# Attention: value products in two parts, bank work at the end of a unit, and two unread products ahead of each piece

## The chip, the cores and the metric

The kernel runs on one core of one Trainium2 chip. The metric is the device time of one execution in microseconds (us), lower is better; three runs were taken of the kernel before.

## The reference, cut to what matters

The input x has 16 batches of 512 tokens with 128 features, float32. Three layers follow each other, each with a layer normalisation and a residual sum:

```python
x = x + 0.5 * ffn(layernorm(x))        # routed and shared experts
x = x + attention(layernorm(x))        # 16 heads of 8 features, 512 keys
x = x + 0.5 * ffn(layernorm(x))

def attention(x):                      # b = 16, s = 512
    q, k, v = x @ Wq.T + bq, x @ Wk.T + bk, x @ Wv.T + bv       # 16 heads of 8
    attn = softmax(einsum('bqhd,bkhd->bhqk', q, k) / sqrt(8))
    out = einsum('bhqk,bkhd->bqhd', attn * head_mask, v)
    return out @ Wo.T + bo
```

## The kernel before

The program has a setup, then `ffn`, `attention` and `ffn` one after the other; the change is in `attention` (L743) alone. It writes each engine's instructions out by hand, and semaphores hold the engines together. Nothing is planned by costs: the order is the order of the code.

**Tiling.** A batch (16 of them) is worked in 16 units `u`; a unit is a group `g = u // 4` of four heads and a block `t = u % 4` of 128 keys (or, for the maxima, of 128 queries). A unit has two halves, and a half has two heads. Scores are needed twice: once with the queries on the partitions, so that VectorE can take each row's maximum (`score_max`, L933, called M here; `take_max`, L1252), and once with the keys on the partitions, for the exponentials (`score_exp`, L919, called E here; `exponential` on ScalarE, L1093). The maxima run 8 units (`AHEAD`) before the exponentials. Each E or M of a half is two TensorE products that use 24 or 26 rows in each of two row tiles of the array; the M of a half uses the two row tiles that the E of the same half doesn't use (`HALVES`). The scores go through three PSUM buffers of two banks in turn (`score_bank`, `bank_free`, L826 to L835): the E of a half waits for the maximum of two halves ago, the M of a half for the exponential of the half before it.

**Value products.** `times_values` (L947) multiplies the four heads' exponentials of a unit with their values, each head in its own 32 columns of the array (`tile_position=(0, h * COLS)`), and sums in the PSUM bank `p_o` over the four blocks of a group. It is one unit behind E. In float32 each of the four products shows as two MATMUL records. When a group is done, ScalarE copies `p_o` out (`copy_o`, L1099), and the first value products of the next group wait for that copy (`o_copied`, L952).

**The shared bank.** All other work of TensorE goes through one PSUM bank `p_x`, in a fixed order of uses (`X_USES`): per batch three transposes of the maxima plus one for the next batch (`turn_max`, L964), four transposes of the sums `o0` to `o3` (`turn_o`, L971), `norm` (`turn_norm`, L979), `out` (`project_out`, L985), `v` (`project_v`, L912) for the next batch, and `x`, `q`, `k` (`turn_x` L897, `project_qk` L904) for the batch after that. Such a use is called a piece. Each fills the bank (`x_bank_filled`); an engine empties it (`x_bank_drained`); the next piece waits for that. `pieces` (L1012) gives each piece its unit on TensorE, `pieces` at L1114 (ScalarE) and L1296 (VectorE) the half in which it is emptied. A full batch has 14 pieces; the first has 11, the last but one 11 and the last 9 (`absent`, L802).

**TensorE's order in a unit** (`batch`, L992): E, M and the unit's piece in half 0; E, M and the value products of the unit before in half 1. From L995 on it waits, at the start of a group, for the maxima to have been packed into `q_pack` by GpSimd's DMA (`pack_max`, L1199), and at unit 8 for the packed operands of the next batch. The maxima travel `take_max`, `split_max` (GpSimd, L1188), `turn_max`, `copy_max` (ScalarE, L1087), `pack_max`. SP's queue issues loads, the packing of q and k (`pack_block`, L856) and the store.

```python
for half in range(2):
    score_exp(b, u, half)
    if there(ahead):
        score_max(ahead, v, half)
    if half == 0:
        pieces(b, u, is_first)
    elif u > 0:
        times_values(b, u - 1)
```

Of the kernel before, what the change touches and what calls it, by code (L numbers as in the profile page):

```python
# [742 lines left out]
def attention(nc, w, src, dst):  # L743
# [9 lines left out]
    with ExitStack() as ctx:  # L753
# [140 lines left out]
        def _(pe):  # L894
# [52 lines left out]
            def times_values(b, u):  # L947

                g, t = divmod(u, NT)
                pe.wait_ge(exp_ready, b.count(PAIRS, 2 * (u + 1)))  # L950
                if t == 0:
                    need(pe, o_copied, b.count(NQ, g))  # L952
                if u == 0:
# [38 lines left out]
            def batch(b, is_first, is_last):  # L992
                a, c = b.step(-1), b.step(1)
                for u in range(UNITS):
                    if u % NT == 0:  # L995
                        g = u // NT
                        pe.wait_ge(max_packed[g % 2], b.count(MAX_DMA * NQ // 2, MAX_DMA * (g // 2 + 1)))
                    ahead, v = (b, u + AHEAD) if u + AHEAD < UNITS else (c, u + AHEAD - UNITS)
                    if v == 0 and there(ahead):
                        pe.wait_ge(packed[ahead.par], ahead.half(PACK_DMA, PACK_DMA))  # L1000
                    for half in range(2):
                        score_exp(b, u, half)
                        if there(ahead):
                            score_max(ahead, v, half)
                        if half == 0:
                            pieces(b, u, is_first)
                        elif u > 0:
                            times_values(b, u - 1)
                        elif not is_first:
                            times_values(a, UNITS - 1)  # L1010

            def pieces(b, u, is_first):  # L1012
                a, c, e = b.step(-1), b.step(1), b.step(2)
                if u == 1:
                    turn_max(b, 1, uses(b, "m1"))
                if not is_first:
                    if u == 2:
                        turn_o(a, 3, uses(b, "o3"))
                    if u == 3:
                        turn_norm(uses(b, "norm"))  # L1020
                    if u == 4:
                        project_out(uses(b, "out"))
                if u == 5:
                    turn_max(b, 2, uses(b, "m2"))
                if u == 6:
                    turn_o(b, 0, uses(b, "o0"))
                if u == 7 and there(c):
                    project_v(uses(b, "v"))
                if u == 8 and there(e):
                    turn_x(e, uses(b, "x"))  # L1030
                if u == 9:
                    turn_max(b, 3, uses(b, "m3"))
                if u == 10:
                    turn_o(b, 1, uses(b, "o1"))
                if u == 11 and there(e):
                    project_qk(e, w.wq, uses(b, "q"))
                if u == 12 and there(e):
                    project_qk(e, w.wk, uses(b, "k"))
                if u == 13 and there(c):
                    turn_max(c, 0, uses(b, "m0"))  # L1040
                if u == 14:
# [17 lines left out]
            times_values(end, UNITS - 1)  # L1059
# [5 lines left out]
        def _(act):  # L1065
# [48 lines left out]
            def pieces(b, u, half, is_first):  # L1114
                a, c, e = b.step(-1), b.step(1), b.step(2)
                now = (u, half)
                if now == (1, 0) and not is_first:
                    copy_o(a, 3, uses(a, "o1") + 1)
                if now == (1, 1):
                    copy_max(b, 1, uses(b, "m1"))  # L1120
                if now == (3, 1) and not is_first:
# [3 lines left out]
                if now == (5, 1):  # L1125
                    copy_max(b, 2, uses(b, "m2"))
                if now == (8, 1) and there(e):
                    x_copy(e, uses(b, "x"))
                if now == (9, 0):
                    copy_o(b, 1, 0 if is_first else uses(b, "o3") + 1)  # L1130
                if now == (9, 1):
                    copy_max(b, 3, uses(b, "m3"))
                if now == (10, 0) and there(e):
                    x_high(e, uses(b, "x"))
                if now == (11, 1) and there(e):
                    operand(e, "q", w.bq, uses(b, "q"))
                if now == (12, 0) and there(e):
                    operand_high(e, "q", uses(b, "q"))
                if now == (12, 1) and there(e):
                    operand(e, "k", w.bk, uses(b, "k"))  # L1140
                if now == (13, 0):
                    copy_o(b, 2, uses(b, "o0") + 1)
                if now == (13, 1) and there(c):
                    copy_max(c, 0, uses(b, "m0"))
                if now == (14, 0) and there(e):
                    operand_high(e, "k", uses(b, "k"))
# [99 lines left out]
        def _(dve):  # L1246
# [49 lines left out]
            def pieces(b, now, is_first):  # L1296
                a, c, e = b.step(-1), b.step(1), b.step(2)
                if there(e):
                    if now == (2, 0):
                        norm_stats(e)  # L1300
                    if now == (3, 0):
                        norm_var(e)
                if not is_first:
                    if now == (2, 1):
                        normalise(a, NQ - 1, uses(b, "o3"))
                    if now == (4, 1):
                        residual(a, uses(b, "out"))
                if now == (6, 1):
# [3 lines left out]
                if now == (10, 1):  # L1312
                    normalise(b, 1, uses(b, "o1"))
                if now == (14, 1):
# [86 lines left out]
```

## Time and profile before

| | |
|---|---|
| median of 3 runs | 2099.72 us (2094.6 to 2109.0) |
| the profiled execution: its own time | 2100.33 us |
| its span, first to last instruction | 2098.1 us |
| TensorE busy over the span | 89% |
| VectorE, ScalarE, GpSimd busy | 71%, 59%, 42% |
| granted TensorE clock, mean of the span | 0.929 of full speed |
| attention, from about 652 to 1527 us | 875 us |

The times of single instructions come from the one profiled execution. A MATMUL record's time holds its way through the array too, so records overlap, and what a product costs the engine is read from start to start. In a timeline the bracket at the end of a line gives the engine's idle time before it and what released it; lines merged from several records say so with a count (x2). L12 is line 12 of the kernel before. The granted clock is a share of full speed: 1.00 is 2.4 GHz, 0.50 is 1.2 GHz.

### The profile page before, as it was taken

The numbers are of one execution on the slowest core, as the hardware profiler recorded it, in microseconds if no ns is written. First come the engines' busy times: TensorE is split into PE (matmuls) and PEld (weight loads), VectorE is DVE, ScalarE is ACT, GpSimd is POOL, SyncE is SP. The second block draws the span as 40 slices with busy tenths as digits, with TensorE's granted clock in tenths as the row PEclk, the third lists the DMA queues.
The fourth block names the chain that finished last, engine by engine and source line by source line (L and its number), as shares of the span: only waits on it lengthen the run. The fifth ranks groups of instructions, "written<-read, shape, count | busy, mean of one in ns | idle before, by whom it ended". The sixth has DMA issues, their size and how long they took to land. (4 is left out here: it accounts for less than half of the span.)

```text
span 2098.1 us, 30450 instructions
## 1 busy us (share of the span) xinstructions
PE 1860.1 (89%) x9600; PEld 1108.9 (53%) x9600; DVE 1496.2 (71%) x2379; ACT 1232.2 (59%) x1914; POOL 887.4 (42%) x875
## 2 busy tenths in 40 slices
PE   3999999999937898999999988888859999999999
PEld 2777777777812333333333333333247777777777
DVE  4767777687517878777787777887447768776775
ACT  3566455555513767666676667776635565556654
POOL 2566555655621222222222222221125565556655
PEclk9999999999955989888888889998879999999999
DMA  2000000000032323222223223222010000000000
GB/s 91 21 11 31 27 24 30 10 30 10 16 59 33 47 47 47 47 42 39 41 44 44 41 41 40 53 44 35 12 36 21 31 11 31 20 30 10 30 14 16
DMA packets 43167, 68.57 MB, mean 33 GB/s; under 512 B 9916, under 2 KB 11444, under 8 KB 43060
## 3 DMA queue, kind: packets, MB, share of 16 engines
q1 hardware_dynamic: 38256, 65.15, 15.7%
q0 software_dynamic: 4096, 1.08, 0.3%
q8 instruction: 58, 0.95, 0.2%
q10 hardware_dynamic: 708, 0.98, 0.1%
q14 instruction: 49, 0.40, 0.1%
HBM read 28.36 MB, written 12.58 MB: 20 GB/s over the span
## 5 line engine op out<-in xcount | busy, mean ns | idle before, releaser
L1259 DVE TENSOR_REDUCE attn_neg_max<-attn_p_score 128x2 f32<-128x1024 f32 x512 | 624.8, 1223 | 211.2 <-PE attn_p_score L941 209.1
L572 POOL TENSOR_TENSOR ffn_hid_low<-ffn_hidden,ffn_hid_high 128x512 fp32r<-128x512 f32 x448 | 580.6, 1298 | 454.9 <-ACT ffn_hid_high L512 454.2
L1096 ACT ACTIVATE attn_exps<-attn_p_score 128x1024 f32<-128x1024 f32 x512 | 519.8, 1025 | 286.6 <-PE attn_p_score L927 284.6
L512 ACT ACTIVATE ffn_hid_high<-ffn_hidden 128x512 fp32r<-128x512 f32 x448 | 281.0, 627 | 255.7 <-DVE ffn_hidden L705 254.8
L503 ACT ACTIVATE ffn_silu<-ffn_p_gate 128x512 f32<-128x512 f32 x448 | 264.0, 589 | 207.8 <-PE ffn_p_gate L375 207.5
L698 DVE TENSOR_TENSOR ffn_gated<-ffn_silu,ffn_p_up 128x512 f32<-128x512 f32 x352 | 240.6, 684 | 175.1 <-PE ffn_p_up L375 112.2
L941 PE MATMUL attn_p_score<-k_pack,q_pack 24*128 24x512 f32 x1024 | 283.2, 553 | 57.7 <-ACT attn_exps L1096 33.0
L958 PE MATMUL attn_p_o<-attn_exps,values 128*32 128x512 f32 x2048 | 312.0, 684 | 8.4 <-ACT attn_o_raw L1102 3.3
L927 PE MATMUL attn_p_score<-q_pack,k_pack 26*128 26x512 f32 x1024 | 271.2, 539 | 14.9 <-DMA q_pack<-attn_max_rows 14.6
L927 PEld LDWEIGHTS attn_p_score<-q_pack,k_pack 26*128 26x128 f32 x1024 | 101.4, 198 | 314.7 <-issue 207.5
L705 DVE TENSOR_TENSOR ffn_hidden<-ffn_gated,ffn_p_spread 128x512 f32<-128x512 f32 x352 | 241.2, 685 | 14.9 <-PE ffn_p_spread L416 4.1
L373 PE MATMUL ffn_p_y<-ffn_hid_high,down_high 128*128 128x512 f32 x448 | 186.3, 416 | 34.0 <-POOL ffn_hid_low L572 33.3
L373 PE MATMUL ffn_p_gate<-ffn_xt_high,gate_high 128*128 128x512 f32 x448 | 188.5, 421 | 0.0
L1203 POOL DMA_DIRECT2D q_pack<-attn_max_rows x128 | 74.3, 582 | 265.0 <-ACT attn_max_rows L1090 265.0
L373 PE MATMUL ffn_p_up<-ffn_xt_high,up_high 128*128 128x512 f32 x448 | 180.4, 403 | 2.9 <-DVE ffn_gated L698 2.8
L375 PE MATMUL ffn_p_up<-ffn_xt_low,up_high 128*128 128x512 f32 x448 | 177.5, 396 | 0.0
L375 PE MATMUL ffn_p_gate<-ffn_xt_low,gate_high 128*128 128x512 f32 x448 | 177.2, 396 | 0.0
L375 PE MATMUL ffn_p_y<-ffn_hid_low,down_high 128*128 128x512 f32 x448 | 177.1, 395 | 0.0
L374 PE MATMUL ffn_p_gate<-ffn_xt_high,gate_low 128*128 128x512 f32 x448 | 176.7, 394 | 0.0
L374 PE MATMUL ffn_p_up<-ffn_xt_high,up_low 128*128 128x512 f32 x448 | 176.2, 393 | 0.0
L374 PE MATMUL ffn_p_y<-ffn_hid_high,down_low 128*128 128x512 f32 x448 | 175.4, 391 | 0.0
L941 PEld LDWEIGHTS attn_p_score<-k_pack,q_pack 24*128 24x128 f32 x1024 | 103.9, 201 | 114.9 <-ACT attn_exps L1096 90.6
(146 smaller groups left out, 2220.9 us busy)
## 6 DMA issues: line engine op xcount, KB each, us to landing
q_pack<-attn_q_high SPq DMA_DIRECT2D x128, 64.0 KB
k_pack<-attn_k_high SPq DMA_DIRECT2D x128, 64.0 KB
ffn_x_in<-in_x SPq DMA_DIRECT2D x16, 256.0 KB, 2.8
ffn_x_res<-in_x SPq DMA_DIRECT2D x16, 256.0 KB, 2.8
after_ffn<-ffn_x_out SPq DMA_DIRECT2D x16, 256.0 KB, 2.0
attn_x_in<-after_ffn SPq DMA_DIRECT2D x16, 256.0 KB, 4.6
k_pack<-attn_k_low SPq DMA_DIRECT2D x64, 64.0 KB
q_pack<-attn_q_low SPq DMA_DIRECT2D x64, 64.0 KB
```

The costliest lines, as they stand in the source:

```text
L373: nc.tensor.matmul(out, weights[0], high, start=start, stop=False)
L374: nc.tensor.matmul(out, weights[1], high, start=False, stop=False)
L375: return nc.tensor.matmul(out, weights[0], low, start=False, stop=stop)
L503: nc.scalar.activation(silu[f % 2][0:n, :], p_gate[f % 2][0:n, :], ACT.Silu).then_inc(silu_ready, 1)
L512: nc.scalar.activation(hid_high[s][0:n, :], hidden[s][0:n, :], ACT.Copy).then_inc(high_ready, 1)
L572: nc.gpsimd.tensor_tensor(hid_low[s][0:n, :], hidden[s][0:n, :], hid_high[s][0:n, :].bitcast(F32), ALU.subtract).then_inc(low_ready, 1)
L705: V.tensor_tensor(hidden[slot(b, f)][:], gated[f % 2][:], p_spread[:], ALU.mult).then_inc(weighted_ready, 1)
L927: last = nc.tensor.matmul(score_bank("exp", b, n)[:, i, :], pack["k"][b.par][rows, g, t * P:(t + 1) * P], pack["q"][b.par][rows, g, :], st ...
L941: last = nc.tensor.matmul(score_bank("max", b, n)[:, j % 2, :], pack["q"][b.par][rows, g, t * P:(t + 1) * P], pack["k"][b.par][rows, g, :] ...
L958: last = nc.tensor.matmul(p_o[h * COLS:(h + 1) * COLS, :], values[b.par][:, t, g * QUAD + h, :], exps[(2 * u + h // 2) % len(exps)][:, h % ...
L1096: nc.scalar.activation(exps[n % len(exps)][:], score_bank("exp", b, n)[:], ACT.Exp, scale=inv_sqrt)\
L1259: V.tensor_reduce(neg_max[g % 2][:, j:j + 2, t], score_bank("max", b, n)[:], AX.X, ALU.max, negate=True).then_inc(max_read, 1)
```

## The change

In `attention`:

- `times_values` takes a half: the two products of heads 0 and 1 of the group come in half 0 and those of heads 2 and 3 in half 1. Each half waits for its own exponential alone; the wait for `o_copied` stands ahead of half 0.
- Every piece moves from half 0 of its unit to the end of half 1 of the unit before (L1012), behind that half's value products, and so comes half a unit earlier in the order.
- `keep_busy`, new, comes ahead of each piece of the table `at`: it waits until the bank `p_x` is empty for that piece and issues two products of 128 x 128 by 128 x 512 (fp32r) from the FFN's weights into it. Nobody reads them; the piece overwrites them.
- ScalarE, VectorE: the copies that empty the bank move half a unit or a unit forward.

Its core (of the moves on ScalarE and VectorE some are left out; the order of the rest is the same):

```diff
@@ -944,22 +944,23 @@
-            def times_values(b, u):
+            def times_values(b, u, half):
                 g, t = divmod(u, NT)
-                pe.wait_ge(exp_ready, b.count(PAIRS, 2 * (u + 1)))
-                if t == 0:
+                pe.wait_ge(exp_ready, b.count(PAIRS, 2 * u + half + 1))
+                if t == 0 and half == 0:
                     need(pe, o_copied, b.count(NQ, g))
...
-                for h in range(QUAD):
+                for h in (2 * half, 2 * half + 1):
                     last = nc.tensor.matmul(p_o[h * COLS:(h + 1) * COLS, :],
                                             values[b.par][:, t, g * QUAD + h, :],
                                             exps[(2 * u + h // 2) % len(exps)][:, h % 2, :], start=t == 0, stop=t == NT - 1,
                                             tile_position=(0, h * COLS))
-                last.then_inc(pv_done, 1)
+                if half == 1:
+                    last.then_inc(pv_done, 1)
@@ -1002,43 +1003,59 @@
                         score_exp(b, u, half)
                         if there(ahead):
                             score_max(ahead, v, half)
-                        if half == 0:
+                        if u > 0:
+                            times_values(b, u - 1, half)
+                        elif not is_first:
+                            times_values(a, UNITS - 1, half)
+                        if half == 1:
+                            keep_busy(b, u, is_first)
                             pieces(b, u, is_first)
-                        elif u > 0:
-                            times_values(b, u - 1)
-                        elif not is_first:
-                            times_values(a, UNITS - 1)
+
+            def keep_busy(b, u, is_first):
+                at = {0: "m1", 4: "m2", 5: "o0", 8: "m3", 9: "o1", 13: "o2"}
+                if not is_first:
+                    at |= {1: "o3", 2: "norm", 3: "out"}
+                if there(b, 1):
+                    at |= {6: "v", 12: "m0"}
+                if there(b, 2):
+                    at |= {7: "x", 10: "q", 11: "k"}
+                if u in at:
+                    pe.wait_ge(x_bank_drained, uses(b, at[u]))
+                    for _ in range(2):
+                        nc.tensor.matmul(p_x[:], w.up[0][:, 0:P], w.gate[0][:, 0:S], start=True, stop=True)

             def pieces(b, u, is_first):
-                if u == 1:
+                if u == 0:
                     turn_max(b, 1, uses(b, "m1"))
...
-                if u == 5:
+                if u == 4:
                     turn_max(b, 2, uses(b, "m2"))
-                if u == 6:
+                if u == 5:
                     turn_o(b, 0, uses(b, "o0"))
...
@@ -1114,36 +1132,34 @@
-                if now == (1, 0) and not is_first:
-                    copy_o(a, 3, uses(a, "o1") + 1)
-                if now == (1, 1):
+                if now == (1, 0):
+                    if not is_first:
+                        copy_o(a, 3, uses(a, "o1") + 1)
                     copy_max(b, 1, uses(b, "m1"))
-                if now == (3, 1) and not is_first:
+                if now == (3, 0) and not is_first:
                     copy_ot(uses(b, "norm"))
                 if now == (5, 0):
                     copy_o(b, 0, 0 if is_first else uses(a, "o2") + 1)
-                if now == (5, 1):
                     copy_max(b, 2, uses(b, "m2"))
-                if now == (8, 1) and there(e):
+                if now == (8, 0) and there(e):
                     x_copy(e, uses(b, "x"))
...
@@ -1296,22 +1312,22 @@
-                    if now == (2, 0):
+                    if now == (1, 0):
                         norm_stats(e)
-                    if now == (3, 0):
+                    if now == (2, 1):
                         norm_var(e)
...
-                    if now == (2, 1):
+                    if now == (2, 0):
                         normalise(a, NQ - 1, uses(b, "o3"))
-                    if now == (4, 1):
+                    if now == (4, 0):
                         residual(a, uses(b, "out"))
-                if now == (7, 1) and there(c):
+                if now == (7, 0) and there(c):
                     copy_values(c, uses(b, "v"))
...
```

## Rows read from the trace of the kernel before

**Rows 1.** The page's first line, the whole program

```profile
span 2098.1 us, 30450 instructions
```

**Rows 2.** Windows: attention, and one stretch of it (length, busy by engine, granted clock)

```profile
core 0: us, PE busy (x) PEld busy (x) DVE busy (x) ACT busy (x) POOL busy (x), PEclk, DMA share, GB/s
652.00:1527.00 875.00, 779.48 (x4822) 289.99 (x4818) 663.15 (x807) 594.13 (x736) 216.44 (x350) 0.89 0.26 40
759.00:776.10 17.10, 17.03 (x75) 5.78 (x74) 11.03 (x21) 8.45 (x11) 4.20 (x6) 0.50 0.55 69
```

**Rows 3.** Timeline, TensorE and ScalarE, a unit without a piece at full clock

```profile
1360.69 0.50 PE L927 MATMUL attn_p_score<-q_pack,k_pack 26*128 26x512 f32 x2
...
1361.23 1.94 ACT L1096 ACTIVATE attn_exps<-attn_p_score 128x1024 f32<-128x1024 f32 x2 [0.59 <-PE attn_p_score L927]
...
1362.31 0.50 PE L941 MATMUL attn_p_score<-k_pack,q_pack 24*128 24x512 f32 x2 [0.71 <-ACT attn_exps L1096]
...
1362.73 1.06 PE L958 MATMUL attn_p_o<-attn_exps,values 128*32 128x512 f32 x8
...
1363.73 0.50 PE L927 MATMUL attn_p_score<-q_pack,k_pack 26*128 26x512 f32 x2
```

**Rows 4.** Timeline, TensorE and ScalarE, around the copy of a group's sums

```profile
1342.26 1.02 ACT L1096 ACTIVATE attn_exps<-attn_p_score 128x1024 f32<-128x1024 f32 x1
...
1342.49 0.27 PE L967 MATMUL attn_p_x<-ident,attn_max_parts 128*32 128x128 f32 x1
...
1342.69 0.50 PE L927 MATMUL attn_p_score<-q_pack,k_pack 26*128 26x512 f32 x2
...
1343.18 0.59 ACT L1102 ACTIVATE attn_o_raw<-attn_p_o 128x512 f32<-128x512 f32 x1
...
1343.92 1.07 PE L958 MATMUL attn_p_o<-attn_exps,values 128*32 128x512 f32 x8
```

**Rows 5.** Timeline, TensorE, other kinds of piece at full clock

```profile
1336.15 1.16 PE L915 MATMUL attn_p_x<-wv,attn_xt 128*128 128x128 f32 x8 [0.37 <-DVE attn_o_norm L1277]
...
1337.24 0.50 PE L927 MATMUL attn_p_score<-q_pack,k_pack 26*128 26x512 f32 x2
...
1345.35 0.66 PE L975 MATMUL attn_p_x<-ident,attn_o_raw 128*128 128x128 f32 x4
...
1345.94 0.50 PE L927 MATMUL attn_p_score<-q_pack,k_pack 26*128 26x512 f32 x2
...
1348.93 0.47 PE L907 MATMUL attn_p_x<-attn_xt_high,wq_high 128*128 128x512 f32 x1 [0.47 <-DVE attn_o_norm L1277]
...
1349.24 0.40 PE L908 MATMUL attn_p_x<-attn_xt_high,wq_low 128*128 128x512 f32 x1
...
1349.47 0.40 PE L909 MATMUL attn_p_x<-attn_xt_low,wq_high 128*128 128x512 f32 x1
...
1349.80 0.50 PE L927 MATMUL attn_p_score<-q_pack,k_pack 26*128 26x512 f32 x2
```

**Rows 6.** One tile, `attn_p_o`: the value products' records

```profile
L958 PE MATMUL attn_p_o<-attn_exps,values x2048: 588/617/1063, 652.4 to 1521.4; 128*32 128x512 f32 x187
```

**Rows 7.** Timeline, TensorE, units at half clock

```profile
759.14 1.94 PE L958 MATMUL attn_p_o<-attn_exps,values 128*32 128x512 f32 x8
...
761.01 0.79 PE L927 MATMUL attn_p_score<-q_pack,k_pack 26*128 26x512 f32 x2
...
761.74 0.39 PE L967 MATMUL attn_p_x<-ident,attn_max_parts 128*32 128x128 f32 x1
...
765.51 0.79 PE L927 MATMUL attn_p_score<-q_pack,k_pack 26*128 26x512 f32 x2
```

**Rows 8.** Waits of TensorE in attention (in total, times, longest)

```profile
PE attn_p_score L927 <- DMA q_pack<-attn_max_rows: 11.2, 7, 3.2
PE attn_p_x L907 <- DVE attn_o_norm L1277: 6.6, 14, 0.5
...
PE attn_p_x L901 <- DVE values L1265: 4.8, 14, 0.4
```

**Rows 9.** Timeline, TensorE, after long idle times

```profile
1273.44 0.50 PE L927 MATMUL attn_p_score<-q_pack,k_pack 26*128 26x512 f32 x2 [2.59 <-DMA q_pack<-attn_max_rows]
...
1275.38 0.79 PE L927 MATMUL attn_p_score<-q_pack,k_pack 26*128 26x512 f32 x2
...
1513.36 1.93 PE L958 MATMUL attn_p_o<-attn_exps,values 128*32 128x512 f32 x8 [1.83 <-ACT attn_o_raw L1102]
```

More of the change, by code:

```diff
@@ L945, in score_max @@
                 last.then_inc(max_tile, 1)
-            def times_values(b, u):
+            def times_values(b, u, half):
                 g, t = divmod(u, NT)
-                pe.wait_ge(exp_ready, b.count(PAIRS, 2 * (u + 1)))
-                if t == 0:
+                pe.wait_ge(exp_ready, b.count(PAIRS, 2 * u + half + 1))
+                if t == 0 and half == 0:
                     need(pe, o_copied, b.count(NQ, g))
-                if u == 0:
+                if u == 0 and half == 0:
                     first_batch = isinstance(b.j, int) and b.k == 0
@@ L1022, in pieces @@
                         project_out(uses(b, "out"))
+                if u == 4:
+                    turn_max(b, 2, uses(b, "m2"))
                 if u == 5:
-                    turn_max(b, 2, uses(b, "m2"))
-                if u == 6:
                     turn_o(b, 0, uses(b, "o0"))
-                if u == 7 and there(c):
+                if u == 6 and there(c):
                     project_v(uses(b, "v"))
-                if u == 8 and there(e):
+                if u == 7 and there(e):
                     turn_x(e, uses(b, "x"))
+                if u == 8:
+                    turn_max(b, 3, uses(b, "m3"))
@@ L1031, in pieces @@
                 if u == 9:
-                    turn_max(b, 3, uses(b, "m3"))
-                if u == 10:
                     turn_o(b, 1, uses(b, "o1"))
+                if u == 10 and there(e):
+                    project_qk(e, w.wq, uses(b, "q"))
                 if u == 11 and there(e):
-                    project_qk(e, w.wq, uses(b, "q"))
-                if u == 12 and there(e):
                     project_qk(e, w.wk, uses(b, "k"))
-                if u == 13 and there(c):
+                if u == 12 and there(c):
@@ L1058, in _ @@
             every_batch(pe, batch)
-            times_values(end, UNITS - 1)
+            times_values(end, UNITS - 1, 0)
+            times_values(end, UNITS - 1, 1)
             turn_o(end, NQ - 1, last_uses)
@@ L1124, in pieces @@
                     copy_o(b, 0, 0 if is_first else uses(a, "o2") + 1)
-                if now == (5, 1):
                     copy_max(b, 2, uses(b, "m2"))
+                if now == (8, 0) and there(e):
+                    x_copy(e, uses(b, "x"))
                 if now == (8, 1) and there(e):
-                    x_copy(e, uses(b, "x"))
+                    x_high(e, uses(b, "x"))
                 if now == (9, 0):
                     copy_o(b, 1, 0 if is_first else uses(b, "o3") + 1)
-                if now == (9, 1):
                     copy_max(b, 3, uses(b, "m3"))
-                if now == (10, 0) and there(e):
-                    x_high(e, uses(b, "x"))
+                if now == (11, 0) and there(e):
+                    operand(e, "q", w.bq, uses(b, "q"))
                 if now == (11, 1) and there(e):
-                    operand(e, "q", w.bq, uses(b, "q"))
+                    operand_high(e, "q", uses(b, "q"))
                 if now == (12, 0) and there(e):
-                    operand_high(e, "q", uses(b, "q"))
+                    operand(e, "k", w.bk, uses(b, "k"))
                 if now == (12, 1) and there(e):
-                    operand(e, "k", w.bk, uses(b, "k"))
+                    operand_high(e, "k", uses(b, "k"))
                 if now == (13, 0):
                     copy_o(b, 2, uses(b, "o0") + 1)
[L1143 to L1146, printed above, removed]
+                    if there(c):
+                        copy_max(c, 0, uses(b, "m0"))
             begin, end = Turn(0, 0), Turn(0, NB - 1)
```

14 lines of the change are left out of this document (7 added, 7 removed).

## The prediction, made before the change was run

> **What bounds the kernel now.** The page gives a span of 2098.1 us [rows 1]; the profiled execution took 2100.33, so 2.2 us lie around the span, and its time is 0.6 above the median of 2099.72. The change touches attention alone, so I read windows next: attention takes 875 us at a mean granted clock of 0.89 [rows 2]. The clock has two levels, 1.00 and 0.50, so it stood at 0.50 for (1 - 0.89) / 0.50 = 0.22 of that time, 193 us, in stretches such as that of 17.1 us from 759.0 [rows 2].
>
> The timeline then shows what a unit waits for. In one without a piece, at full clock, E starts at 1360.69, its exponential at 1361.23 (0.54 later), M of half 1, which waits for that exponential, at 1362.31 (1.62), the value products at 1362.73 (2.04), the next unit's E at 1363.73: 3.04 us [rows 3]. So the unit is a loop through two engines: E, exponential, M, value products, E. The 1.00 us of the products is on it. In half 0 TensorE is idle for part of the 1.62 us, and most pieces lie there now. At half clock the same unit takes 765.51 - 761.01 = 4.50 us [rows 7], a loss of 0.32 of the time.
>
> Does this explain the 875 us? 256 units x 3.04 = 778; 6 us from the last value product (its record starts at 1521.4 [rows 6]); waits for the bank and for `q_pack`, 11.2 us and five of 4.8 to 6.6, some 38 together [rows 8]; and 193 x 0.32 = 62 at half clock. The sum is 884, within about 1%. I build on this loop.
>
> **Part 1, value products in two parts.** The 2048 records are 588 to 617 ns each, and eight of them (four heads, two records each) take 1.06 us from first start to last end [rows 3, 6]. One head alone, two records in a row, would take about as long, so the four heads run side by side. Two heads then take as long as four: I price a half at the 1.00 us from its start to the next E. From below, a price per head would give 0.50. I take 1.00, since the records' lengths speak for it. The half in half 0 starts when M does and is over 1.43 after E, ahead of the 1.62 at which M of half 1 can start: hidden there, as long as nothing else lies in that place. The half in half 1 costs its 1.00, as the whole did. A unit without a piece stays at 3.04.
>
> The Trainium skill weighs in here (TensorE: Matmul & The Clock Gate, Part 3: Packing small matmuls): it has packed tiles gain less than their number, 2.38 times for three column tiles. By that a group of two would be a little cheaper than one of four, and some 20 us would go from the sum (an estimate); no run here shows two alone.
>
> **Part 2, pieces at the end of half 1.** They leave the place that half 0 gave them and follow the value products, right ahead of the next E: in the loop, uncovered. Their prices, first record to next E: transposes 0.59 (1345.35 to 1345.94), `v` and `out` 1.09 (1336.15 to 1337.24), `q` and `k` 0.87 (1348.93 to 1349.80) [rows 5], maxima 0.20 (1342.49 to 1342.69) [rows 4]. Counts over 16 batches: 92 of four transposes (`o0` to `o2` 48, `o3` and `norm` 30, `x` 14), 30 of `v` and `out`, 28 of `q` and `k`, 63 of maxima. 92 x 0.59 + 30 x 1.09 + 28 x 0.87 + 63 x 0.20 = 124 us. From below 0, if the loop had slack behind the value products; rows 3 show none, so I take all of it. What goes: the 38 us of waits [rows 8], since each bank is emptied in the following half 0, on VectorE or ScalarE about 2.4 after E, and wanted at 3.04. (They are left out of the loop already, so nothing is subtracted twice.) The maxima's way through GpSimd and its two DMAs starts half a unit earlier and the four units that it has are longer, so I expect no `q_pack` wait; if that cover fails it costs the old 11 us. ScalarE's and VectorE's moved copies queue behind one exponential or one maximum, with half a unit to spare. SP's store and loads wait for events that come earlier in the order; nobody is late for them.
>
> **Part 3, two unread products ahead of each piece.** 92 + 30 + 28 + 63 = 213 pairs. A product of this kind costs 0.23 from start to start (1349.24 to 1349.47) [rows 5], 0.46 a pair: 98 us, in the loop as well. From above a pair with its own entry costs 0.31 + 0.23 = 0.54 [rows 5], 17 us more. From below 0, if it filled a wait for the bank; but those are gone, so 98.
>
> The Trainium skill (TensorEngine Tiling (Array Packing), Tiling Modes) says that changing the tiling mode drains the engine. The unread products follow column-tiled ones, an order that the trace of before lacks. By the rule some 0.2 us for each pair, about 40 us, could come on top (an estimate); by the row, whose 1.00 ends in such a change already, nothing.
>
> **Part 4, a new wait.** `copy_o` stays behind the exponential of half 0, at units 1, 5, 9 and 13, but the value products that wait for it now stand in half 0 of the same unit, ahead of E and M of half 1. The copy starts at 0.54 + 1.02 (the exponential), takes 0.59, and products follow its end by 0.15 (1343.18 + 0.59 to 1343.92) [rows 3, 4]: they start 2.30 after E instead of 0.43. Queued behind them are half 1's E and M, and with these ScalarE and VectorE. The unit becomes 2.30 + 1.00 + 0.42 + 1.00 = 4.72, 1.68 more. It happens 4 x 16 - 1 = 63 times: 106 us. Below: 0, if the copy came in time. Above: the 1.83 that such a wait took at 1513.36 [rows 9]. I take 1.68.
>
> **Part 5, the clock.** At full clock attention would take 778 + 124 + 98 + 106 + 6 = 1112 us, 237 more than 875. At half clock a unit is bound by TensorE: scores 0.73 and products 1.87 [rows 7], twice: 5.20 against 3.04, a loss of 0.42 of the time spent so. The unread products fill TensorE, but the copy waits leave it idle for 1.8 us four times a batch, and the clock fell after a wait of 2.59 (scores at 0.50 at 1273.44, 0.79 at 1275.38) and at one of 1.83 (value products 1.93 at 1513.36) [rows 9]. Also no pair stands in units 14, 15 and most of 0. So I expect half clock in some 0.12 of attention, between 0 and the 0.22 of before: 1112 / (1 - 0.12 x 0.42) = 1171 us, 296 more. 2098.1 + 296 + 2.2 = 2396; less the 0.6 to the median: **2395 us**.
>
> **Rivals.**
> - The clock is held throughout: 2100 + 237 = 2337. For it: the change adds 98 us of products over the whole array. Against: rows 9. The Trainium skill (TensorE: Matmul & The Clock Gate, HAM oscillation — how this bites in real kernels) says that sustained work keeps the clock up; by that this case would win. Chance 0.18.
> - The unread products don't do what they are for, and half clock takes 0.22 to 0.35 of attention: 1225 to 1304 us, so 2450 to 2529. Chance 0.15.
> - A half is priced by the head, 0.50. With price p attention takes 256 x (2.04 + p) + 63 x (0.68 + p) + 228 = 793 + 319 p: 952 us at 0.50, 1002 with half clock as in the forecast, so 2227. Against it are the overlapping records [rows 6]. Chance 0.14.
> - Not slower: scores of the next half start under the value products, whose halves leave half of the columns free, so that only p = 0.2 stays on the loop: 793 + 64 = 857, 18 less, 2082. It decides from p = 0.26, where 793 + 319 p is 875. For it: E and M share the array by row tiles. Against: no score starts inside a group of value products in rows 3, and pieces, pairs and copy waits still have to be won back. Chance 0.06.
>
> **How the numbers follow.** The forecast has 0.47, with a range of its own from 2340 to 2450. To hold 8 in 10 the range reaches down to the case of the price by head and up past 0.22 of half clock: 2215 to 2480. About 1% is what a measurement of this kernel tells from no change. Faster by over 1% and within 1% come from the fourth rival alone with some doubt around it: 0.04 and 0.03; slower 0.93.
>
> **What would show it.** Right: the unread products in the list of lines as 426 matmuls near 0.4 us each; value products still near 0.6 a record, in groups of four records that take 1.0; the next E some 0.5 + the piece's price after them; among TensorE's waits, value products on the copy of `p_o`, 63 times about 1.8; bank waits gone; VectorE and ScalarE with longer waits for scores; the batch near 70 us at full clock. Wrong: groups of two heads in half the time (part 1), the copy wait short or absent (part 4), units with a piece near 3 us (part 2 and the loop), granted clock in attention at 1.00 or below 0.85 (part 5), or any change in the two FFNs.

## The result, and the profile after

The change makes the kernel slower: median 2376.36 us of 4 runs (2372.57 to 2384.22) against 2101.63 of 4 runs of the kernel before, a ratio of 1.131 (95% interval 1.126 to 1.136). The forecast was 2395, with a range of 2215 to 2480. The profiled execution took 2372.57 us, its span is 2370.4. The ratios and intervals in this document leave out runs over 1.5% above the fastest of the same kernel, so they can differ a little from the quotient of two medians.

The windows of after that answer to [rows 2]: attention, and what lies on both sides of it.

```profile
core 0: us, PE busy (x) PEld busy (x) DVE busy (x) ACT busy (x) POOL busy (x), PEclk, DMA share, GB/s
652.00:1799.00 1147.00, 1038.41 (x5250) 377.67 (x5246) 665.41 (x807) 608.94 (x737) 216.68 (x350) 0.96 0.19 31
...
0.00:652.00 652.00, 552.43 (x2413) 415.37 (x2428) 432.10 (x812) 327.53 (x600) 347.23 (x276) 0.95 0.12 31
1799.00:2370.40 571.40, 527.71 (x2336) 403.48 (x2352) 400.37 (x761) 309.69 (x577) 323.81 (x249) 0.97 0.07 23
```

Attention takes 1147 us instead of 875, 272 more, and that is the whole difference: the parts beside it are 652 and 571 us long. TensorE is busy for 1038 us of it, VectorE for 665 against 663 and ScalarE for 609 against 594 [rows 2]: these two do nearly the same work and wait longer for it. The granted clock rose from 0.89 to 0.96.

The timeline of after shows one unit with all that is new. TensorE's and ScalarE's lines of unit 9, from its E (1119.56) to that of unit 10 (1125.25):

```profile
1119.56 0.49 PE L927 MATMUL attn_p_score<-q_pack,k_pack 26*128 26x512 f32 x2
...
1120.09 1.02 ACT L1114 ACTIVATE attn_exps<-attn_p_score 128x1024 f32<-128x1024 f32 x1 [0.83 <-PE attn_p_score L927]
1121.01 0.59 ACT L1120 ACTIVATE attn_o_raw<-attn_p_o 128x512 f32<-128x512 f32 x1
...
1121.75 1.05 PE L958 MATMUL attn_p_o<-attn_exps,values 128*32 128x512 f32 x4 [1.69 <-ACT attn_o_raw L1120]
...
1122.73 0.50 PE L927 MATMUL attn_p_score<-q_pack,k_pack 26*128 26x512 f32 x2
...
1123.17 1.05 PE L958 MATMUL attn_p_o<-attn_exps,values 128*32 128x512 f32 x4
...
1124.15 0.73 PE L1027 MATMUL attn_p_x<-gate_high,up_high 128*128 128x512 f32 x2
1124.72 0.60 PE L976 MATMUL attn_p_x<-ident,attn_o_raw 128*128 128x128 f32 x4
1125.25 0.50 PE L927 MATMUL attn_p_score<-q_pack,k_pack 26*128 26x512 f32 x2
```

Read it from start to start. Four records of two heads take 0.98 (1121.75 to 1122.73 and 1123.17 to 1124.15), where eight records of four heads took 1.00 [rows 3]. The first half waits 1.69 for the copy of the sums, which ScalarE starts behind its exponential. The two unread products take 0.57 and the transposes behind them 0.53, right ahead of the next E. The unit is 5.69 us long.

TensorE's waits inside attention, answering to [rows 8]:

```profile
PE attn_p_o L958 <- ACT attn_o_raw L1120: 81.2, 48, 1.7
PE attn_p_o L958 <- ACT attn_exps L1114: 24.7, 15, 1.7
PE attn_p_x L976 <- ACT attn_o_raw L1120: 0.7, 1, 0.7
```

The 48 and the 15 are the 63 waits that part 4 counted: the 15 of some 1.65 stand in unit 1, where ScalarE runs exponential and copy in the same order. The products follow the end of the copy there too (copy to 723.52, products from 723.62), though the profile names the exponential. Together they are 106 us. The waits for the bank and for `q_pack` of [rows 8] are gone.

### The profile page after: what moved, and what is told of

Same layout as the page of the kernel before. It is cut to its first block and busy times, and to the rows that moved or that the text cites. A ratio compares the mean times of both kernels' runs of the same rounds, so it can differ in the third digit from the quotient of the medians.

```text
span 2370.4 us, 31271 instructions
## 1 busy us (share of the span) xinstructions
PE 2118.6 (89%) x9995; PEld 1196.5 (50%) x10026; DVE 1497.9 (63%) x2379; ACT 1246.2 (53%) x1914; POOL 887.7 (37%) x875
## 5 line engine op out<-in xcount | busy, mean ns | idle before, releaser
L958 PE MATMUL attn_p_o<-attn_exps,values 128*32 128x512 f32 x2048 | 563.2, 629 | 106.0 <-ACT attn_o_raw L1120 81.2
L941 PE MATMUL attn_p_score<-k_pack,q_pack 24*128 24x512 f32 x1024 | 264.4, 516 | 17.4 <-DMA k_pack<-attn_k_high 12.2
L927 PE MATMUL attn_p_score<-q_pack,k_pack 26*128 26x512 f32 x1024 | 261.5, 507 | 3.3 <-DMA q_pack<-attn_max_rows 3.3
L927 PEld LDWEIGHTS attn_p_score<-q_pack,k_pack 26*128 26x128 f32 x1024 | 96.4, 185 | 309.2 <-issue 293.1
L958 PEld LDWEIGHTS attn_p_o<-attn_exps,values 128*32 128x32 f32 x2048 | 76.5, 109 | 238.6 <-ACT attn_exps L1114 127.1
L1210 POOL TENSOR_TENSOR attn_max_parts<-attn_neg_max,zeros 128x16 fp32r<-128x16 f32 x64 | 13.9, 218 | 466.8 <-DVE attn_neg_max L1275 466.8
```

What stands on the lines that cost most here:

```text
L927: last = nc.tensor.matmul(score_bank("exp", b, n)[:, i, :], pack["k"][b.par][rows, g, t * P:(t + 1) * P], pack["q"][b.par][rows, g, :], st ...
L941: last = nc.tensor.matmul(score_bank("max", b, n)[:, j % 2, :], pack["q"][b.par][rows, g, t * P:(t + 1) * P], pack["k"][b.par][rows, g, :] ...
L958: last = nc.tensor.matmul(p_o[h * COLS:(h + 1) * COLS, :], values[b.par][:, t, g * QUAD + h, :], exps[(2 * u + h // 2) % len(exps)][:, h % ...
```

## The experiments

A median is given beside its ratio to the kernel before, run on the same chip. Each window, wait and timeline comes from the one profiled execution of its kernel. In the expectations, the loop theory is the sum of parts 1 to 4 of the prediction, at a given clock; the clock theory adds what a change of the granted clock would give or take. The window of attention goes from 652 us to the end of its last residual sum on VectorE, and its columns are those of the windows of after.

### e1: without the unread products

```diff
                         if half == 1:
-                            keep_busy(b, u, is_first)
                             pieces(b, u, is_first)
```

> The change without the unread products (426 matmuls left out), all else as in the change. Loop theory: each pair stands uncovered ahead of the next scores; a pair and its piece took 1124.15 to 1125.25 in the trace of after, the pair 0.57 of it, so 213 x 0.57 = 121 us go: 2376 - 121 = 2255 us if the clock stays at its mean of 0.96 in attention. Clock theory on top: the pairs are what holds the clock; without them half clock takes about the 0.22 of attention that it had before, attention is 993 / (1 - 0.22 x 0.42) = 1094 us instead of 1147, and the time is about 2323 with a mean clock near 0.89. Rival (the pairs fill idle time): within 15 us of 2376.

Measured: 2301.58 us (2291.93 to 2307.74), ratio 1.098 (1.090 to 1.105). The 75 us that go are less than the 102 that the same products cost where the clock stays at 1.00 (e12 to e2, below): here the clock of attention falls from 0.96 to 0.93. Attention, and a stretch of it about a batch long with many falls:

```profile
652.00:1718.70 1066.70, 957.93 (x4822) 305.49 (x4818) 665.13 (x807) 608.81 (x737) 216.54 (x350) 0.93 0.21 33
...
927.00:998.00 71.00, 64.28 (x312) 20.61 (x310) 43.63 (x55) 38.71 (x48) 14.51 (x23) 0.88 0.22 35
```

The clock of 0.93 lies between the two forms of the loop theory, and so does the time. The unread products cost time and, in a kernel with the copy waits, give part of it back.

### e2: the copy of the sums ahead of the exponential

```diff
                     for half in range(2):
+                        if half == 0:
+                            group_copy(b, u, is_first)      # copy_o of units 1, 5, 9, 13
                         exponential(b, 2 * u + half)
                         pieces(b, u, half, is_first)
...
```

with the four copies taken out of `pieces`.

> The change with ScalarE's copy of a group's sums (copy_o) ahead of the exponential of half 0 instead of behind it, at units 1, 5, 9, 13. Loop theory: the sums are ready at the end of the unit before, so the copy runs beside the pair and the piece, and the 63 waits of 1.7 us go; a unit with a copy (5.69 us) becomes like one without (4.13): 63 x 1.56 = 98 us less, 2278, and some 15 less again if the half-clock stretches of 3.4 us, which come just after a copy wait, go too: 2263. Rival (the wait only takes the place of another, for the exponential or a score bank): 2360 to 2376 and the same total of TensorE waits under another name.

Measured: 2238.82 us (2237.68 to 2239.10), ratio 1.067 (1.060 to 1.074): 138 less than the change, and more than the 113 expected. The waits are gone and not replaced, and no stretch of its attention is at half clock but its first 3.8 us and its last 2.9:

```profile
652.00:1665.70 1013.70, 1010.39 (x5246) 378.89 (x5244) 664.34 (x807) 613.61 (x737) 217.61 (x350) 1.00 0.22 35
```

So moving one ScalarE instruction by one place is worth 133 us of attention: about 98 for 63 waits (worked out below) and the rest, 35, for the clock. The rival is refuted.

### e3: all four heads in half 1 again

```diff
-                        if u > 0:
-                            times_values(b, u - 1, half)
-                        elif not is_first:
-                            times_values(a, UNITS - 1, half)
                         if half == 1:
+                            for part in range(2):
+                                if u > 0:
+                                    times_values(b, u - 1, part)
+                                elif not is_first:
+                                    times_values(a, UNITS - 1, part)
                             keep_busy(b, u, is_first)
                             pieces(b, u, is_first)
```

> The change with all four heads' products in half 1, as before it; pieces, pairs and copies as in the change. Loop theory: the half in half 0 was hidden ahead of M of half 1, so putting it back costs and saves nothing by itself, but the copy of the sums is then in time but for some 0.15 us: 63 x 1.5 = 95 less, 2281; the granted clock could fall, since TensorE is idle in each half 0 again: with 0.15 of attention at half clock about 2320. Rival (the split itself is what made TensorE the bound, 256 x 1.0 us more work of which half shows): 2376 - 128 - 95 = 2150.

Measured: 2290.89 us (2275.81 to 2300.85), ratio 1.093 (1.085 to 1.101), between the two numbers of the loop theory; the rival's 2150 is far off. In the fastest of its four runs, the profiled one, attention takes 1050.9 us at a clock of 0.96, though only two copy waits are left (3.5 us in all):

```profile
652.00:1702.90 1050.90, 832.72 (x5251) 340.72 (x5250) 664.38 (x807) 586.17 (x737) 216.99 (x350) 0.96 0.21 33
...
1104.90:1115.20 10.30, 9.07 (x33) 3.14 (x34) 5.08 (x8) 3.96 (x6) 1.15 (x2) 0.50 0.56 66
```

This kernel differs from e2 in that TensorE is idle in half 0 until M of half 1 can start: 247 waits for the exponential, 207.7 us. It has all the unread products, and yet it falls to half clock in stretches such as that of 10.3 us; within e2's attention there is none.

### e4: the unread products alone, in the kernel before

```diff
                         if half == 0:
+                            keep_busy(b, u, is_first)    # two products ahead of each piece, as in the change
                             pieces(b, u, is_first)
```

> The kernel before with two unread products ahead of each piece in its old place in half 0, and nothing else. Loop theory: scores 0.43, pair 0.57 and piece 0.53 end at 1.53, ahead of the 1.62 at which M of half 1 can start, so pairs ahead of transposes and maxima are hidden; v and out (30) cost 0.37, q and k (28) 0.16, and behind the 56 or so waits for the bank a pair costs up to its 0.57: +45 us. Clock theory: half clock falls from 0.22 of attention to 0.05: -48 us. Together about 2100, mean clock of attention 0.97. If the pairs are hidden but the clock doesn't answer: 2147. If they are not hidden and the clock answers: 2101 + 121 - 48 = 2174.

Measured: 2102.48 us (2095.98 to 2107.74, 10 runs), ratio 1.004 (1.000 to 1.008): the loop theory's number. Attention takes 874 us at 0.98, against 875 at 0.89:

```profile
652.00:1526.00 874.00, 793.08 (x5248) 346.15 (x5246) 662.39 (x807) 601.59 (x736) 216.67 (x350) 0.98 0.26 40
```

The products did what they are for, the clock rose, and the price took all of it back. The timeline shows one place where:

```profile
1116.90 0.50 PE L941 MATMUL attn_p_score<-k_pack,q_pack 24*128 24x512 f32 x2
1117.75 0.73 PE L1024 MATMUL attn_p_x<-gate_high,up_high 128*128 128x512 f32 x2 [0.35 <-DVE values L1279]
1118.32 0.60 PE L901 MATMUL attn_p_x<-ident,attn_xn 128*128 128x128 f32 x4
1118.84 0.50 PE L927 MATMUL attn_p_score<-q_pack,k_pack 26*128 26x512 f32 x2
```

The pair stands behind the wait for the bank, so the wait isn't filled, and the piece is late by the pair's 0.57.

### e5: the move of the pieces alone

This is e3 without the unread products.

```diff
                         if half == 1:
                             ...
-                            keep_busy(b, u, is_first)
                             pieces(b, u, is_first)
```

> The change without its unread products (left out) and with all value products in half 1: what is left is the move of the pieces to the end of half 1, and of the copies behind them. Loop theory: all 213 pieces stand in the loop at 0.59, 1.09, 0.87 and 0.20: attention at full clock 778 + 124 + 6 = 908 us, so 2133; with the 0.22 of half clock that the kernel before had, at a loss of about 0.35, 984 and 2209. Rival (a piece costs the same wherever it stands, so the move only removes the 38 us of waits for the bank): 2062 to 2101.

Measured: 2186.59 us (2177.24 to 2196.09), ratio 1.042 (1.034 to 1.049).

```profile
652.00:1607.10 955.10, 739.59 (x4820) 272.88 (x4818) 662.87 (x804) 584.40 (x735) 215.93 (x350) 0.93 0.24 37
```

955 us at 0.93: (1 - 0.93) / 0.50 = 0.14 at half clock. At the loss of 0.32 that the prediction read for a unit of the kernel before, 955 x (1 - 0.14 x 0.32) = 912 would be left at full clock; at its 0.42 for a unit bound by TensorE, 899. The 778 + 124 + 6 = 908 of the prediction lies between, but this working is too coarse to test it; e12 does. The move by itself makes the kernel slower; its rival (2062 to 2101) is refuted.

### e6: the halves alone, in the kernel before

```diff
                         if half == 0:
                             pieces(b, u, is_first)
-                        elif u > 0:
-                            times_values(b, u - 1)
-                        elif not is_first:
-                            times_values(a, UNITS - 1)
+                        if u > 0:
+                            times_values(b, u - 1, half)
+                        elif not is_first:
+                            times_values(a, UNITS - 1, half)
```

with `times_values` of the change and e2's `group_copy`.

> The kernel before with the value products in two halves, and copy_o ahead of the exponential of its half, so that the first half doesn't wait for it; pieces stay in half 0, ahead of that half's products; no unread products. Loop theory: a unit without a piece or with a maximum's transpose stays at 3.04; one with four transposes becomes 3.43 (+0.39, 92 times), with v or out +0.89 (30), with q or k +0.67 (28): +82 us at equal clock, 2183, and 2111 to 2150 if the clock is held better because TensorE is idle less. Rival (two more groups' worth of work show in full, 256 x 0.99): about 2350. Rival (price by the head, 0.50): within 15 us of 2101.

Measured: 2176.49 us (2175.56 to 2177.78), ratio 1.036 (1.029 to 1.042). The clock is at 1.00, but the time is near the 2183 expected at an unchanged clock: for a clock held better, 2111 to 2150 had been expected.

```profile
652.00:1603.10 951.10, 908.31 (x4822) 302.82 (x4818) 664.27 (x807) 608.43 (x736) 216.25 (x350) 1.00 0.24 37
```

Its timeline shows two costs that the expectation had left out, in the unit from 1056.15:

```profile
1056.15 0.50 PE L927 MATMUL attn_p_score<-q_pack,k_pack 26*128 26x512 f32 x2
...
1057.02 0.27 PE L968 MATMUL attn_p_x<-ident,attn_max_parts 128*32 128x128 f32 x1 [0.17 <-ACT attn_k_full L1081]
1057.51 1.05 PE L958 MATMUL attn_p_o<-attn_exps,values 128*32 128x512 f32 x4 [0.22 <-ACT attn_o_raw L1104]
1058.49 0.50 PE L927 MATMUL attn_p_score<-q_pack,k_pack 26*128 26x512 f32 x2
```

Half 1 starts 2.34 after E (1056.15 to 1058.49), against the 1.62 counted: the waits for the bank (the transpose starts 0.87 after E, not 0.43), which had lain in idle time, push the half behind them now, and the copy is still 0.22 late. The two rivals (2350, and within 15 us of no change) are both refuted.

### e7 and e8: the bank emptied early, without and with the unread products

```diff
-                    if now == (2, 1):
+                    if now == (2, 0):
                         normalise(a, NQ - 1, uses(b, "o3"))
-                    if now == (4, 1):
+                    if now == (4, 0):
                         residual(a, uses(b, "out"))
...
-                if now == (1, 1):
+                if now == (1, 0):
                     copy_max(b, 1, uses(b, "m1"))
```

and the same for `normalise` of `o0` to `o2` and for `copy_values`, with `norm_stats` moved from half 0 of unit 2 to half 0 of unit 1, in the kernel before; e8 adds e4's `keep_busy`.

> The kernel before, with VectorE emptying the bank in the half in which it is filled (behind the first maximum of the unit, not the second), and the copy of m1 half a unit earlier. Loop theory: the five waits for the bank of 4.8 to 6.6 us, 27 together, go, and some of the 11 for q_pack: 2101 - 30 = 2070 at equal clock. Rival (VectorE's maxima come later by what now stands ahead of them, and TensorE waits for score banks instead): 2095 to 2110, with waits of the scores on VectorE in their place.

> As e7, with two unread products ahead of each piece in half 0. Loop theory with the clock: pairs ahead of transposes and maxima lie before 1.62 and are hidden now that the bank is empty in time; v and out cost 0.37, q and k 0.16, +16 us; half clock falls to 0.05 or less of attention, -48: about 2040, under both kernels. Rival (the pairs delay the next transposes as in e4): 2075 to 2100.

Measured: e7 2092.07 us (2066.11 to 2115.37, 12 runs), ratio 0.991 (0.987 to 0.995); e8 2076.50 (2068.54 to 2085.29, 6 runs), ratio 0.988 (0.983 to 0.993). The windows of e7, then of e8:

```profile
652.00:1522.70 870.70, 796.58 (x4818) 293.72 (x4816) 663.00 (x806) 596.77 (x735) 215.87 (x350) 0.87 0.25 40
```

```profile
652.00:1505.80 853.80, 808.14 (x5248) 349.24 (x5246) 665.78 (x807) 600.42 (x736) 216.40 (x350) 0.95 0.26 41
```

In e7 the waits of TensorE on VectorE's copies, 27 us, are gone. The rival's waits of scores on VectorE did not come; those of M for the exponential grew from 32.3 us in 54 waits to 43.6 in 86. Some 13 to 19 us of the expected 30 came, by the medians (the kernel before has 2105.23 on this chip) or by the ratio. In the profiled execution the clock of attention is 0.87, but over all runs the mean granted clock of the span is 0.927 against 0.930, so the clock does not explain what is missing, and the cause stays open. In e8 the clock is at 0.95 instead of the expected 0.98 or more, and the time is in the range of its rival (2075 to 2100), though the rival's waits for the bank are not there. Both are a little faster than the kernel before, by 1%; their intervals overlap, so which of the two is better stays open.

### e9, e10, e11: halves where they are hidden

e9 is e7 with halves in the units 15 and 0, which have no piece; e10 has them in 1, 5, 9 and 13 too, with e2's `group_copy`; e11 adds unread products ahead of the 92 pieces of four transposes.

```diff
+HEAD_PARTS = ((0, 1), (2, 3))
+SPLIT = (15, 0)                     # e10, e11: (15, 0, 1, 5, 9, 13)
...
+                        if u in SPLIT:
+                            heads = HEAD_PARTS[half]
+                        elif half == 1:
+                            heads = (0, 1, 2, 3)
+                        else:
+                            continue
```

> e7 (the kernel before with the bank emptied early), and the value products in two halves in units 15 and 0 alone, which have no piece. Loop theory: the first half (0.43 to 1.42 after E) lies ahead of the 1.62 at which M of half 1 starts, so it costs nothing. Clock theory from e2 and e6 (products in halves held the clock at 1.00 without a single fall in their attention, with and without unread products): the falls after unit 14 go; a batch at full clock took 50 to 52 us in e7, and its 55 to 58 us batches were those with half clock: 2092 - 16 x 0.22 x 52 x 0.32 = 2034 if all half clock goes, 2050 if two thirds. Rival (the halves hold the clock only where every unit has them, or it needs the unread products): 2080 to 2100, with the falls where e7 has them.

> e9 with halves also in the units of a maximum's transpose (1, 5, 9, 13) and copy_o ahead of the exponential there. Loop theory: 0.43 + 0.20 + 0.99 = 1.62, just hidden, so no cost; the clock has six of sixteen units with more work: 2030, at or under e9. Rival (the bound is crossed and each such unit loses 0.1 to 0.3): 6 to 19 us over e9 at the same clock.

> e10 with two unread products ahead of the 92 pieces of four transposes alone (184 matmuls), none ahead of v, out, q, k and the maxima. Loop theory: 0.43 + 0.57 + 0.53 = 1.53 is ahead of 1.62, hidden; if e10 holds the clock already the same time as e10 within 5 us, if not 10 to 30 less. Rival (hidden only on paper, as in e4 and e8): 92 x 0.1 to 0.3, 9 to 28 us over e10.

Measured: e9 2089.44 us (2072.09 to 2112.46), ratio 0.997 (0.993 to 1.002); e10 2080.31 (2067.55 to 2087.22), 0.992 (0.989 to 0.995); e11 2081.96 (2072.70 to 2090.69), 0.993 (0.990 to 0.995). None reached the 2030 to 2050 expected; e9 lies in the range of its rival (2080 to 2100), and those of e10 and e11, each slower than the run before it by 6 us or more, did not come. The windows of e9, of e10 (an execution of 2067.78, at the lower end of its runs) and of e11, the last to its last residual sum:

```profile
652.00:1511.10 859.10, 781.68 (x4820) 286.28 (x4818) 662.41 (x807) 600.82 (x735) 216.64 (x350) 0.93 0.26 41
```

```profile
652.00:1494.50 842.50, 797.18 (x4822) 288.12 (x4818) 661.17 (x807) 607.91 (x735) 216.38 (x350) 0.96 0.26 42
```

```profile
652.00:1499.70 847.70, 809.94 (x5004) 320.21 (x5002) 662.37 (x807) 608.60 (x735) 216.22 (x350) 0.97 0.25 41
```

e9 can't be told from the kernel before. The clock rises with the number of units that have halves, 0.87, 0.93, 0.96 (over the span and all runs 0.927, 0.939, 0.956), but doesn't reach 1.00. The pairs of e11 raised it once more, to 0.964 over the span, and its time is that of e10 within 2 us. What is left in e10 is TensorE's wait for the packed maxima: it has 9 such waits, 22.8 us, and 8 of its stretches at half clock begin within 2.5 us of the end of one. In e9 these waits are longer than in e7, 30.9 us in 20 against 9.3 in 8, which is part of why e9 missed. The waits of e9, those of e10, and a stretch of e10's timeline:

```profile
PE attn_p_score L929 <- DMA q_pack<-attn_max_rows: 30.9, 20, 3.4
```

```profile
PE attn_p_score L929 <- DMA q_pack<-attn_max_rows: 22.8, 9, 4.1
PE attn_p_o L960 <- ACT attn_o_raw L1111: 6.6, 26, 1.0
```

```profile
1040.40 0.50 PE L929 MATMUL attn_p_score<-q_pack,k_pack 26*128 26x512 f32 x2 [2.08 <-DMA q_pack<-attn_max_rows]
...
1041.89 0.79 PE L929 MATMUL attn_p_score<-q_pack,k_pack 26*128 26x512 f32 x2
```

The copy of m1 had been moved for this wait; it did not remove it. What holds the packed maxima up in the DMA queues wasn't tried.

### e12: e2 without the unread products

```diff
-                            keep_busy(b, u, is_first)
```

> e2 (copy_o ahead of the exponential) without the unread products (left out): products in halves and pieces at the end of half 1 remain. Loop theory: 213 pairs less at the 0.57 read in the trace of after, 121 us under e2's 2239: 2118, if the clock stays at 1.00 in attention as in e2 and e6, that is, if it is the halves that hold it. Rival (the unread products hold it, as e1 suggests, where their removal took the mean clock down): half clock in 0.12 to 0.22 of attention, 2118 + 45 to 80 = 2163 to 2200. A piece without a pair ahead may pay its entry of some 0.05, 10 us more in both.

Measured: 2138.44 us (2137.70 to 2140.28), ratio 1.018 (1.012 to 1.023).

```profile
652.00:1563.90 911.90, 893.28 (x4820) 295.12 (x4818) 662.51 (x807) 608.53 (x735) 216.58 (x350) 1.00 0.25 38
```

The clock is 1.00 without a single unread product: with products in halves and no copy wait it holds without them, and the rival is refuted. Attention is 102 us shorter than in e2, 0.48 a pair; the time had been expected at 2118, since 0.57 a pair was taken from the timeline.

## Why the prediction was right

The four kernels e5, e12, e2 and the change form a ladder, and attention gives the price of each step. From e5 to e12 two things change, the halves and the place of the copy; every other step is one edit.

| step | attention, us (clock) | forecast at full clock | measured |
|---|---|---|---|
| pieces to the end of half 1 (e5) | 955 (0.93) | 908 in all | 899 to 912, by the loss taken for the clock |
| products in halves, copy ahead (e12) | 912 (1.00) | 0 more, 908 in all | 912 in all, 4 over |
| unread pairs (e2) | 1014 (1.00) | 98 more | 102 more |
| copy wait (the change) | 1147 (0.96) | 106 more | 133 more: 98 for the waits, 35 for the clock |

**Part 1** held on both counts. Two heads take 0.98 against 1.00 for four, so the price by the head is refuted, and with it the rival of 2227. (The Trainium skill, TensorE: Matmul & The Clock Gate, Part 3: Packing small matmuls, has three column tiles gain 2.38 times; the estimate drawn from it, a group of two a little cheaper than one of four, comes to 0.02 in this trace, some 5 us in all.) The half in half 0 is hidden while a piece doesn't share its place: e12 is 4 us over the 908. Where it does (e6), the halves cost.

**Part 2** held as a sum, 124 us: e12, at full clock, has all of it and ends 4 us from the forecast. Behind a pair a piece is cheaper than it was alone, 0.53 for four transposes against 0.59.

**Part 3** held as a sum and not in its pieces: a pair takes 0.57 from its start to the piece, not 0.46, but it takes over the piece's entry, so the net is 0.48.

**Part 4** was the term least to be seen in the trace of before, and it came out as counted: 63 waits, 106 us of them. A copy unit with transposes is 5.69 us long, one without the copy 4.13 (norm, 1160.53 to 1164.66 in the trace of after), so the net is 1.56, not 1.68, and the 63 cost 98.

The misses of parts 2 to 4 are small, 4 and 4 too low and 8 too high, and cancel: 912 + 102 + 98 = 1112, the forecast's own sum at full clock. That it is met so exactly is luck.

**Part 5** is the one that was mis-sized. At 0.96, some 0.08 of attention is at half clock, and by the prediction's loss 1147 x 0.08 x 0.42 = 39 us go to it (by the ladder 35), where the forecast had 0.12 and 59. That is about what the forecast was too high by, 19 us. The place was right: in each of the 16 batches the clock falls within 1.6 us after the start of the products that waited for the copy in unit 13, and is back 3.4 us later, as here.

```profile
1140.02 1.10 PE L958 MATMUL attn_p_o<-attn_exps,values 128*32 128x512 f32 x4 [1.69 <-ACT attn_o_raw L1120]
...
1141.05 0.79 PE L927 MATMUL attn_p_score<-q_pack,k_pack 26*128 26x512 f32 x2
...
1144.49 0.60 PE L976 MATMUL attn_p_x<-ident,attn_o_raw 128*128 128x128 f32 x4
1145.02 0.50 PE L927 MATMUL attn_p_score<-q_pack,k_pack 26*128 26x512 f32 x2
```

The reason given for it was only half right. The prediction let the unread products fill TensorE and said nothing of the halves. With all pairs and whole products the clock is at 0.96 (e3), with halves and no pair at 1.00 (e12). For the clock to be held throughout, the rival of 2337, the copy wait has to go, as in e2. The drain that the Trainium skill (TensorEngine Tiling (Array Packing), Tiling Modes) names for a change of the tiling mode adds nothing that the loop's 1.00 didn't hold: the pair follows the halves 0.98 after their start (1123.17 to 1124.15), as scores do. The 40 us of that sentence did not come.

The rival on the other side fell at its first condition. No score starts under a half's products in the timeline of after; p is 0.98, far from 0.26. That the clock can be won back is true: by the prediction's estimate, 0.89 to 1.00 is worth some 62 us. The change pays 124 + 102 + 98 us for a part of it.

## What to carry to other kernels

When an instruction is moved ahead in an engine's order, look up what it waits for and where the releaser stands in its own engine's order: here the first value product was moved by half a unit and the copy that releases it was not, which cost 133 us and was mended by moving one call. Idle time of a busy engine is worth something only in the place where it lies; work moved out of it, behind the last thing that the loop waits for, is paid in full (124 us here). Unread work that is to keep a clock up costs its time when it stands behind a wait and ahead of real work (e2, e4); placed into the idle time ahead of the wait it may be free, but no run here tried that.

## What the runs showed of the hardware that was not expected

Value products of two heads at a time, which take as long as those of four, went with a clock of 1.00 in attention wherever every unit had them and no wait of TensorE was over 0.7 us (e2, e6, e12). With four heads side by side it was at 0.87 to 0.93 without the unread products (before, e5, e7) and at 0.95 to 0.98 with them (e3, e4, e8). e5 and e12 compute the same; they differ by the halves and the place of the copy, and in clock by 0.93 to 1.00. I had expected the unread products to be what counts. Whether it is the shape of the halves or that they fill idle time isn't told apart: TensorE's records cover 893 of 912 us in e12 and 740 of 955 in e5. Mere cover isn't all of it: the stretch of [rows 2] is covered for 17.03 of its 17.10 us and stays at half clock.

The clock fell at the 1.7 us wait of unit 13 in all 16 batches of the change, but at only 7 of the 47 equal waits in units 1, 5 and 9. Why these differ wasn't settled. Each fall of the change lasted 3.4 us, while in the kernel before, with four heads side by side, 10 of the 14 stretches that begin inside attention lasted 13.7 to 20.5.
